# A graph layer and a mixture of experts: the node update moved from a stage of its own into the edge loop, and the order of the final adds

## The reference

```python
n = layernorm(x);  x0 = n[:, :64];  x1 = n[:, 64:].reshape(N, 64, 3)
s0, s1 = x0 @ W_sc0 * z / 8, einsum('nuc,uv->nvc', x1, W_sc1) * z / 8      # own part
h0, h1 = the same with W_lin1_0, W_lin1_1                                  # sent along edges
w = silu(ele @ fc_w0 / sqrt(8)) @ fc_w1 / 8                                # 4 x 64 per edge
y = segment_sum(products of w, h[src], sh, by dst) / 4                     # 128 + 128*3 per node
x = x + sin(pi/8) * s + cos(pi/8) * (y @ W_lin2) * z / sqrt(128)
n = layernorm(x)
x = x + shared(n) + sum over the 2 best of 8 experts of gate * expert(n)   # 256 -> 1024 -> 256, gelu
```

## Time and profile before

| | us |
|---|---|
| median of 3 runs (1191.36 to 1194.25) | 1193.81 |
| the profiled execution's own time | 1192.31 |
| its span | 1190.3 |
| mean granted clock of PE, of full speed | 0.971 |
| PE busy | 1043.2 |
| PEld / DVE busy | 915.6 / 750.4 |
| ACT / POOL busy | 727.2 / 633.0 |
| node stage | 0 to 57 |
| edge stage | 57 to 566 |
| update stage | 566 to 656 |
| shared expert | 656 to 804 |
| routed experts | 804 to 1190 |

### The profile page before, as it was taken

How to read it: one execution, slowest core, us unless ns; L and a number is a source line. 1 busy time by engine, 2 the same in 40 slices (tenths; PEclk the granted TensorE clock), 3 DMA queues, 4 the chain that set the end, 5 groups by cost and what they waited for, 6 DMA issues and landing times. The chain is left out here.

```text
span 1190.3 us, 30949 instructions
## 1 busy us (share of the span) xinstructions
PE 1043.2 (88%) x8929; PEld 915.6 (77%) x8929; DVE 750.4 (63%) x1842; ACT 727.2 (61%) x2353; POOL 633.0 (53%) x645
## 2 busy tenths in 40 slices
PE   3788988889998988887688999988999999999991
PEld 2567777777777777776565999988999999899991
DVE  6566677766666667775476764445666656657561
ACT  3778888888888888886355645544444443444430
POOL 4077777777777777774000044442455455455552
PEclk9979999999999999999898999998999999999996
DMA  5233333343333433434554522323243444433221
GB/s 161 94 111 109 109 111 109 109 111 108 110 110 107 111 108 109 110 108 147 161 178 177 177 90 89 102 81 118 49 111 81 85 107 112 86 74 77 41 50 22
DMA packets 91911, 125.57 MB, mean 105 GB/s; under 512 B 29278, under 2 KB 70670, under 8 KB 91712
## 3 DMA queue, kind: packets, MB, share of 16 engines
q0 software_dynamic: 31792, 67.29, 22.9%
q1 hardware_dynamic: 56128, 54.01, 14.6%
q10 hardware_dynamic: 3920, 3.41, 0.8%
HBM read 98.30 MB, written 26.36 MB: 105 GB/s over the span
## 5 line engine op out<-in xcount | busy, mean ns | idle before, releaser
L568 ACT ACTIVATE hots<-hot,sh_st 128x64 f32<-128x64 f32 x1568 | 384.9, 334 | 0.2 <-issue 0.2
L711 PE MATMUL psY<-prod,hots 128*64 128x128 f32 x2352 | 279.4, 276 | 0.0
L707 PE MATMUL psY<-prod,hots 128*64 128x256 f32 x784 | 220.6, 401 | 52.1 <-DVE prod L615 52.1
L711 PEld LDWEIGHTS psY<-prod,hots 128*64 128x64 f32 x2352 | 256.0, 138 | 0.0
L543 POOL DMA_INDIRECT x_wlo<-h_tab,src_sb x224 | 214.2, 956 | 70.1 <-issue 70.1
L1738 ACT ACTIVATE q_hf<-q_psA,x_b 128x256 f32<-128x256 f32 x232 | 110.0, 474 | 191.9 <-PE q_psA L1282 186.5
L1683 POOL DMA_INDIRECT out_rows<-q_ob,q_index x58 | 119.9, 2068 | 136.1 <-DMA out_rows<-q_ob,q_index 89.2
L543 POOL DMA_INDIRECT rows<-h_tab,src_sb x168 | 161.0, 958 | 51.2 <-issue 51.2
L707 PEld LDWEIGHTS psY<-prod,hots 128*64 128x64 f32 x784 | 83.2, 136 | 91.0 <-DVE prod L615 89.4
L1282 PE MATMUL q_psA<-q_xhi,x_whi 128*128 x464 | 132.4, 285 | 9.4 <-DVE q_xlo L1776 9.0
L1869 PE MATMUL q_psB<-x_whi,q_hhi 128*128 128x256 f32 x464 | 133.0, 287 | 0.1
(11 more groups left out here) (212 smaller groups left out, 2281.2 us busy)
## 6 DMA issues: line engine op xcount, KB each, us to landing
x_raw<-in_w SPq DMA_DIRECT2D x18, 1024.0 KB, 5.8
x_wlo<-h_tab,src_sb POOLq DMA_INDIRECT x224
x_sb<-in_x SPq DMA_DIRECT2D x5, 640.0 KB, 5.4
h_tab<-x_sb ACTq DMA_DIRECT2D x5, 640.0 KB, 3.2
u_x<-in_x SPq DMA_DIRECT2D x5, 640.0 KB, 7.0
xnew_d<-u_x SPq DMA_DIRECT2D x5, 640.0 KB, 3.5
xn_d<-u_xn SPq DMA_DIRECT2D x5, 640.0 KB, 5.1
s_xnew<-xnew_d SPq DMA_DIRECT2D x5, 640.0 KB, 5.5
```

The lines of the kernel that those rows point to most:

```text
L568: ins = nc.scalar.activation(hots[p][:, c, n, :], hot[p][:, c, :], ACT.Copy, scale=sh_st[p][:, 4 * c + n:4 * c + n + 1])
L707: nc.tensor.matmul(psY[p][0:SPAN, 0:FEAT], hots[p][:, c, 0, :], prod[p][:, c, 0:4, :].rearrange("p a u -> p (a u)"), start=(c == 0), stop= ...
L711: ins = nc.tensor.matmul(side[:, k::3 - k, :][:, 0:2, :], hots[p][:, c, k + 1, :], prod[p][:, c, 4::k + 1, :][:, 0:2, :], start=(c == 0 an ...
```

## The change

1. `update_block` is gone. Its work on a pair of tiles is cut in pieces and put into the edge loop, which now runs in turns of eight steps (`ITER`); turn k fetches, turns and mixes pair k-1 and finishes pair k-2. The last three tiles follow the last edge step as one batch.
2. Its input: POOL adds x to s in `node_block` and SP stores the sum (`base_d`); the edge stage loads two tiles of it and of y at a time. All of sh is loaded at once. The ring of rows has four buffers in place of seven, psE and psW one each in place of two. `rounds` grows by one if some step's first node lies below the limit that the early update needs.
3. The update normalises on ACT (`Identity` with scale and bias); the inverse root is three Newton steps on DVE in place of ACT's square root.
4. The shared expert's weights are loaded at the end of `node_block`; their high parts are made in turn 1, their low parts in eight pieces at the start of `shared_block`. The shared groups run 0 to 4 (before: 4 first). The slot scatters are spread over 15 points of a group in place of 13.
5. `routed_block`: `landed(d - 1, 1)` stands ahead of `rows_of`; for the last expert PE does all down products of tile s-1 ahead of the up products of s (`apart`), and DVE writes the output of s-1 in tile s (`early`, `late`).

```diff
@@ edge_block, DVE
+            def graph_result(r, p, i):
+                dve.wait_ge(mixed, r * NT + t + 2)
+                if i == 0:
+                    dve.wait_ge(rows_free, r * (LAST + 1) + p + 1)
+                nc.vector.scalar_tensor_tensor(out=xnew[:, i, :], in0=psM[i if tail else 0], scalar=zo[:, at(t)],
+                    in1=x_end[:, i, :] if tail else x_st[:, i, :], op0=ALU.mult, op1=ALU.add).then_inc(xnew_done, 1)
+                dve.wait_ge(xnew_done, r * NT + t + 2)
+                nc.vector.bn_stats(stats[:, i, :], xnew[:, i, :]).then_inc(stats_done, 1)
+            def turn_of(r, k, q, done=None, at_work=None):
+                j = k * ITER + q
+                add_y(r, j - 2, q % 2)
+                one_hot(r, j + 1, (q + 1) % 2)
+                if done is not None and q == 0:
+                    graph_result(r, done, 1)
+                if done is not None and q in (1, 2):
+                    variance(r, done, q - 1)        # 2 aggregations and 12 small operations in all
+                products(r, k, j, q)
+                if done is not None and q == 7:
+                    low(r, done)
+                if at_work is not None and q == 6:
+                    graph_result(r, at_work, 0)
@@ edge_block, PE
             def radial(r, j, p):
                 pe.wait_ge(silu_done, r * T + j + 1 + 2)
-                pe.wait_ge(prod_done, (r * T + j) * 2 + 2 * RING - 2)
+                pe.wait_ge(prod_done, (r * T + j) * 2 + 2 * RING)
+            def turn_of(r, k, q, done=None, at_work=None):
+                hidden(r, k + (q + 2) // ITER, (q + 2) % ITER)
+                radial(r, j + 1, (q + 1) % 2)
+                segment(r, j, q % 2)
+                if done is not None and q == 4:
+                    turn_x(r, done)
+                if done is not None and q == 6:
+                    score(r, done)
+                if at_work is not None and q == 3:
+                    pe.wait_ge(y_in, 32 * (r * IN_LOOP + at_work + 1))
+                    turn(r, at_work * PAIR, y_st[:, 0:2, :])
+                if at_work is not None and q == 5:
+                    mix(r, at_work * PAIR)
+                    turn(r, at_work * PAIR + 1, y_st[:, 2:4, :])
+                if at_work is not None and q == 7:
+                    mix(r, at_work * PAIR + 1)
@@ edge_block, ACT (behind silu and scale_hot of the step)
+                if done is not None and q == 3:
+                    normalize(r, done)              # 2 x (64 and 192 columns), Identity
+                if done is not None and q == 5:
+                    copy_columns(r, done)
+                if done is not None and q == 7:
+                    copy_logits(r, done)
+                if at_work is not None and q == 4:
+                    copy_sums(r, at_work * PAIR)
+                if at_work is not None and q == 6:
+                    copy_sums(r, at_work * PAIR + 1)
@@ edge_block, SP, each turn k
+                    fetch_y(r, k, k - 1)            # waits for the sum of step 8k
+                    e_load(r, k * 2 + 2, 0)
+                    store_rows(r, k - 2)
+                    rows_stored(r, k - 2)
+                    e_load(r, k * 2 + 3, 1)
+                    store_cols(r, k - 2)
+                    cols_stored(r, k - 2)
@@ node_block, POOL, each tile
+                    pool.tensor_tensor(s_row[:, 0:MUL], s_row[:, 0:MUL], x_row[:, 0:MUL], ALU.add)
+                    pool.tensor_tensor(s_row[:, MUL:].rearrange("p (c u) -> p c u", c=3), ...
+                                       x_row[:, MUL:].rearrange("p (u c) -> p c u", c=3), ALU.add).then_inc(based, 1)
@@ shared_block, DVE
+            for n in range(4):
+                low_weights(n)
             shift()
             dve.sem_inc(hlo_done, 4)
             dve.sem_inc(ob_done, 1)
+            for n in range(4, 8):
+                low_weights(n)
@@ routed_block, POOL
             with pool.Fori(1, all_but_two) as d:
+                landed(d - 1, 1)
                 rows_of(within(d + 4, TILES + 1))
-                landed(d - 1, 1)
                 add(d, 0)
                 landed(d, 0)
                 add(d, 1)
@@ routed_block, PE, tile(s, e, done, fresh, apart)
+                if apart:
+                    for f in range(FC):
+                        down(*done, f, done_side)
                 for f in range(FC):
-                    if done is not None:
+                    if done is not None and not apart:
                         down(*done, f, done_side, fresh)
@@ routed_block, DVE, tile(s, e, done, after, early, late)
+                    if f == 1 and early is not None:
+                        output(*early)
+                    if f == FC - 1 and late is not None:
+                        output(*late)
```

More of the change, by code:

```diff
@@ new lines, in store_cols, with cols_stored @@
+            def store_cols(r, p):
+                n = parts(p)
+                first = sp.snap(p * (PAIR * P)) if not isinstance(p, int) else p * PAIR * P
+                sp.wait_ge(lo_done, r * (LAST + 1) + p + 2)
+                sp.sem_inc(u_go, 1)
+                for h, part in enumerate((xhi, xlo)):
+                    sp.dma_start(xT_d[h, :, :, at(first, n * P)], part[:, :, 0:n * P].bitcast(F32)).then_inc(cols_out, 16)
+            def cols_stored(r, p):
+                sp.wait_ge(cols_out, 32 * (r * (LAST + 1) + p + 1))
+                sp.sem_inc(cols_free, 1)
@@ L672, in _ @@
                 add_y(r, T - 2, 0)
                 add_y(r, T - 1, 1)
+                variance(r, ITERS - 2, 1)
+                dve.wait_ge(x_end_in, 16)
+                for i in range(MOST):
+                    graph_result(r, LAST, i)
+                low(r, ITERS - 2)
+                variance(r, LAST, 0)
+                variance(r, LAST, 1)
+                low(r, LAST)
         @block.tensor
         def _(pe):
-            R = pe.value_load(rounds_i[0:1, 0:1], min_val=1, max_val=BLOCKS + 1)
@@ new lines, in _ @@
+            with pe.Fori(0, R) as r:
+                hidden(r, 0, 0)
+                hidden(r, 0, 1)
+                radial(r, 0, 0)
+                for q in range(ITER):
+                    turn_of(r, 0, q)
+                pe.wait_ge(w_ready, 1)
+                for q in range(ITER):
+                    turn_of(r, 1, q, None, 0)
+                with pe.Fori(2, ITERS) as k:
+                    for q in range(ITER):
+                        turn_of(r, k, q, k - 2, k - 1)
+                turn_of(r, ITERS, 0)
+                turn_of(r, ITERS, 1)
+                pe.wait_ge(y_done, (r + 1) * T + 2)
+                first = LAST * PAIR
+                for i in range(MOST):
+                    turn(r, first + i, y_sb[:, 2 * (first + i):2 * (first + i) + 2, :], i)
+                for i in range(MOST):
+                    mix(r, first + i, i)
+                turn_x(r, ITERS - 2)
+                score(r, ITERS - 2)
+                turn_x(r, LAST)
+                score(r, LAST)
@@ L1390, in _ @@
             sp.wait_ge(ob_done, NT + 1)
[L1391 removed]
+            store((NG - 1) * GROUP)
         @block.gpsimd
@@ L1803, in output, with tile @@
                                             None, ALU.mult).then_inc(ob_done, 1)
-            def tile(s, e, done=None, after=None):
+            def tile(s, e, done=None, after=None, early=None, late=None):
                 high(s, 0)
@@ L1902, in _ @@
                 tile(within(first + 1), e, (first, e), e > 0)
-                further(pe, n, first, lambda s, e=e: tile(s, e, (within(s - 1), e)))
+                further(pe, n, first, lambda s, e=e: tile(s, e, (within(s - 1), e), apart=e == EXPERTS - 1))
             last = within(first + n - 1)
```

839 lines of the change are left out of this document (418 added, 421 removed).

## The result

The changed kernel takes 1232.4 us (median of 4, 1230.8 to 1232.9), the kernel before 1192.6 in the same comparison: ratio 1.033 (95% interval 1.031 to 1.035). The profiled execution has a span of 1230.9 against 1190.3: **+40.6 us**. The forecast was +22. The direction holds, and three of the five parts lie within the ends given for them; the edge stage (+63.2, ends 0 and +60) was taken too small, and the weights (-1.6, ends 0 and +6) came out on the other side of zero.

A forecast was written before the change was run, and what follows sets the result against it. The bound was taken to change by stage: gathers in the edge stage, PE in the shared, POOL's adds in the routed. Terms 3 + 35 - 67 + 3 + 48 = +22 on 1192.3 gave 1214, median 1215; own range 1198 to 1232.

The forecast's parts named there:

- Update stage: Between last sum and shared expert: 90.8 us gone, a final batch of 24 us stays; -67 (-73 to -57).
- Edge stage: Edge loop with the spread update: a turn of 43.75 us against POOL's 40.24; +35 over ten full turns (0 to +60).
- Rival A: Edge stage keeps POOL's pace, rows stay the bound, its place being piece 0 of each turn; 1180 us, chance 0.19.
- C: Rival: more is late in the edge stage, y behind piece 3 or POOL's ring of four dry; 1245 us, chance 0.12.
- Piece 0: First step of an edge turn: its products wait behind the second result and its mix, ending 8.35 us after S7.
- S7: Zero point of the edge-turn estimate: when PE starts behind the products of piece 7.
- The two steps behind it: Pieces 1 and 2 of an edge turn, with DVE's small operations of 1.6 and 1.25 us: ends at 13.5 and 18.35.
- The other five: Pieces 3 to 7 of an edge turn: PE leads at 4.52 us each plus small additions, ending at 43.75.
- Turn 1: Edge turn ahead of the ten full turns; the forecast's +35 covered only the ten full ones.
- Node stage: POOL adds x to s; one more addition and a longer store behind the last s tile: +3, worse end +20.
- Weights, shared: Start of the shared stage: eight subtractions on DVE make PE wait for the first low part; +3 (0 to 6).
- Adds: Routed experts: copies and gathers no longer lie under the landing, 1.9 us a tile; +48 (33 to 66).

The follow-up runs named there:

- e1: Changed kernel with only the second result of a pair moved behind the products of piece 0 in the vector queue: 1195.1 us, 0.9985 of the kernel before.
- e4: Changed kernel with ten unread products on PE in its stand-still at piece 0 of each full turn: 1224.7 us, 1.023 of the kernel before.
- e3: Kernel before with only the wait for the second add's landing put ahead of copies and gathers: 1438.0 us, 1.020 of the kernel before.
- e7: Changed kernel with both results moved, routed stage as before and first expert's weights loaded later: 1154.2 us, 0.965 of the kernel before.
- e2: Changed kernel with the whole routed stage as before the change: 1411.4 us, 0.9996 of the kernel before, on the chip where that takes 1412.

## Why the prediction was right, and where it was short

1. *Update stage.* Right: 26.2 for 24, within 18 to 34.
2. *Edge stage.* The mechanism is right, and e1 shows it: the result in front of the products, waiting for the mix behind segment 7. Rival A (the stage keeps POOL's pace) fell at its named place. The time lies between the forecast's 1215 and C's 1245, but neither of C's reasons shows: from 160 to 460 us no row has PE waiting for y (L1072), nor DVE for gathered rows. The size failed in four terms. (a) Piece 0: 8.35 forecast, 9.55 measured. S7 was set at the end of products 7 (292.1), but PE was still at the scores of the pair (L1110, to 292.8) and had the next hidden product (L1035) to do, so its radial product starts at 293.34. +1.2. (b) The two steps behind it: 10.0 forecast, 11.6 measured on average. The halved clock is 0.8 of it (e4), and DVE's small operations, with their handovers, the other 0.8 (2.0 and 1.7 for 1.6 and 1.25). The clock stood in no term, though the chain that I worked out had PE waiting for 3 us. (c) The other five: 25.4 forecast, 24.8 measured. Together 45.9 for 43.75, +21 over ten turns. (d) Turn 1 has one result of its own and was counted as free, +6.3, and the load at the boundary of the stages had no term at all, +3.
3. *Node stage.* Near: +4.3 for +3. The term itself held: from the end of the last s tile to the first instruction of the edge stage it is 6.3 us for 3.3. The other 1.3 comes ahead of it. POOL's two additions take 0.33 and 0.67 us a tile (1.0, inside 0.5 to 1.2). The Trainium skill's rule of the exclusive port pair ("SBUF - State Buffer", SBUF: two separate sides) would have given 10, which is 7 more than my term. The trace agrees with its direction: DVE's conversion of 392 elements (L357), which runs while POOL adds, takes 694 ns for 365. But all that the stage loses ahead of the last s tile is the 1.3. Why so little was not looked into. The groups from 10 to 60 us:

```profile
L304 POOL TENSOR_TENSOR s_sb<-s_sb,x_sb x25 | 16.7, 668 | 0.0
...
L303 POOL TENSOR_TENSOR s_sb<-s_sb,x_sb x25 | 8.3, 332 | 16.9 <-ACT s_sb L422 16.0 <-issue 0.9
```

4. *Weights, shared.* Wrong sign, small: -1.6 for +3. The wait for the first low parts that the term was made of doesn't show: behind its first matmul PE waits twice in this stage, 3.3 and 1.7 us at the end, where the kernel before waited once, 6.2.
5. *Adds.* The order is right and e3 isolates it, but at 0.9 us a tile (24.5 / 28.5), not the 1.9 chosen and below the end of 1.3 that I gave it. The row that I worked from was a quick one (6.2 us from add 1 to add 0, for 6.8 on average), and with the move the adds themselves got quicker (e3), for which I had allowed only part of the step from 2.5 to 1.9. "apart and early bring nothing" is wrong: they cost 10, by the wait of 13.3 us for PE's turn of a later tile. The rest, 4.9, is a first add that comes 32.2 us behind the first up product, for 27.5, and the end. So 24.5 + 9.9 + 4.9 = 39.3 for 48: one term twice too large and two left out, and that the sum comes near is luck. Landing is 3.9 in the median, so the fixed cost of about 2 us that the Trainium skill gives ("DMA: Bandwidth & Descriptors", Anatomy of one DMA), by which the part would be +20 (an estimate), did not decide, although the order's 24.5 alone comes near it.

The total missed 18.6 of 40.6: 28 too little in the edge stage, 9 too much in the routed one, 1 between the others.

The signs that I named came out near, not all inside: the turn is 45.2 to 46.7 us where I gave 43 to 45, DVE waits for psO twice a turn (1.4 and 4.4) where I gave once some 3, and two adds take 13.5 where I gave 14. The 1232.4 lies just above my own range of 1198 to 1232 and inside 1172 to 1246.

Not tried: the early outputs with the old order of POOL, where its copies stand ahead of the adds as well; and what is left above POOL's pace, some 2 us a turn, most of it PE's wait behind DVE's small operations.

## What to carry to other kernels

When work is spread into the slack of a loop, the sums per engine say only whether it can fit. Put each added operation that reads another engine's result where that result is already there, behind the operation that the other engine is waiting for: here one line moved by a step was worth 37 us. Work out what stands still because of an added wait, and price the next few microseconds of PE at the lower clock. A wait for a landing hides nothing unless the independent work is issued ahead of it.

## What the runs showed of the hardware

*The clock falls within the loop.* In nine of the ten full turns the granted clock goes to 0.50 in or behind PE's stand-still of 3.0 us, for three to seven us, and the step from piece 1 to piece 2 takes 5.6 to 7.0. In the first full turn, with the same stand-still ending at 165.8, it stays at 1.00 and the step takes 5.4. With PE busy through the stand-still (e4) it stays at 1.00 in all ten. Windows of the changed kernel, behind the stand-stills of the first and the second full turn:

```profile
165.00:168.00 3.00, 2.20 (x23) 1.82 (x25) 2.75 (x11) 2.21 (x10) 2.32 (x3) 1.00 0.40 119
...
212.00:215.40 3.40, 3.40 (x25) 3.37 (x25) 2.75 (x12) 0.37 (x2) 2.29 (x3) 0.50 0.38 99
```

The Trainium skill describes the same ("TensorE: Matmul & The Clock Gate", HAM oscillation), for waits on DMA; here it is a wait on DVE, and it costs 8 us of 1231.

*A load goes with a late start of a queue that it isn't on.* With the DMA engines at 1.01 from 58 to 68 us, the first gather of POOL, "issue" in the trace, started 7.0 us behind its predecessor. With the load moved away (e7) 4.2 remain, for 2.1 in the kernel before. What POOL waits for there isn't shown.

*On two of the four chips of the experiments PE was fed more slowly.* On them the kernel before takes 1400 to 1412 us. In e3's trace some 216 us are left above the kernel before when the adds' 24.5 are taken off, and 212 of them lie between the first and the last products. From 160 to 460 us its PE waits 45 us for "issue", and the granted clock is 0.87, where the kernel before has no such wait and 1.00. In the edge stage of e3 single matmuls follow one another every 0.72 us:

```profile
309.49 0.27 PE L711 MATMUL psY<-prod,hots 128*64 128x128 f32 x1 [0.46 <-issue]
310.21 0.31 PE L711 MATMUL psY<-prod,hots 128*64 128x128 f32 x1 [0.45 <-issue]
310.93 0.27 PE L711 MATMUL psY<-prod,hots 128*64 128x128 f32 x1 [0.41 <-issue]
```

The adds are as fast there as elsewhere (348.1 us in e2 for 349.6). What slows PE in this one stage was not found; as all runs on these two chips came before those on the other two, it isn't even shown that it is the chip and not the hour. A change is to be judged by its ratio on the same chip, and by a trace that shows the same bound: by the first six runs alone, moving the result would have looked worthless.
